# Adding two bias vectors on TensorE and redrawing five instruction lists in a two-layer transformer kernel

## What is computed

```python
gamma1, gamma2, scale1, scale2, shift1, shift2 = (silu(cond) @ Wada.T + bada)   # 6 x 256
def attn(xin):                                        # 16 heads of 16
    qkv = xin @ Wqkv.T + concat([q_bias, 0, v_bias])
    qn, kn = q / |q| * exp(min(s, log 100)), k / |k|
    p = softmax(qn @ kn.T + attn_bias)
    return (p @ v) @ Wproj.T + bproj
x = x + attn(ln(x) * (scale1 + 1) + shift1) * gamma1
h = gelu((ln(x) * (scale2 + 1) + shift2) @ Wfc1.T + bfc1)        # 1024 wide
x = x + (h @ Wfc2.T + bfc2) * gamma2
```

## Time and profile before

| what | us |
|---|---|
| median of 3 runs | 243.81 (243.23 to 246.11) |
| the profiled execution | 244.3 |
| its span, first to last instruction | 242.4 |
| DVE busy in the span | 201.6 |
| ACT busy | 156.6 |
| POOL busy | 95.3 |
| PE busy / PEld busy | 228.3 / 175.6 |

### The profile page before, as it was taken

How to read it: one execution, slowest core, us unless ns; L and a number is a source line. 1 busy time by engine, 2 the same in 40 slices (tenths; PEclk the granted TensorE clock), 3 DMA queues, 4 the chain that set the end, 5 groups by cost and what they waited for, 6 DMA issues and landing times.

```text
span 242.4 us, 4991 instructions
## 1 busy us (share of the span) xinstructions
PE 228.3 (94%) x1792; PEld 175.6 (72%) x1792; DVE 201.6 (83%) x418; ACT 156.6 (65%) x316; POOL 95.3 (39%) x167
## 2 busy tenths in 40 slices
PE   6999999999999999999999999999999799998982
PEld 2679674575567758567689999999897476867762
DVE  3879889999996997997977998776898988998743
ACT  2430491854899987985989828753608695877930
POOL 7416317028203302380839194234505545550000
PEclk9797999999999999999999999999999999999998
DMA  6970040000000003203000100000000000000112
GB/s 209 329 302 3 1 173 1 3 1 5 3 0 9 0 3 96 85 0 105 34 3 0 47 0 0 3 0 3 0 0 4 0 0 1 3 0 0 47 43 92
DMA packets 3641, 9.75 MB, mean 40 GB/s; under 512 B 536, under 2 KB 920, under 8 KB 3360
## 3 DMA queue, kind: packets, MB, share of 16 engines
q1 hardware_dynamic: 3616, 9.41, 11.3%
...
## 4 chain that ended last, share of the span: by engine, by line
PE 65%; DVE 15%; ACT 6%; issue 5%; POOL 3%; DMA 3%; SPq 1%; POOLq 0%; ACTq 0%; DVEq 0%
PE ring L835 11%; PE ring L841 10%; PE ring L836 10%; PE ring L837 10%; PE pv L944 5%; DVE nm L1223 5%; PE psx L974 5%; PE ring L898 3%; PE pv L1133 2%; PE psx L924 2%; DVE qn L1356 2%; DMA stage_a<-in_wada 2%; PE ring L848 1%; PE psx L1105 1%; DVE qstk L1397 1%
## 5 line engine op out<-in xcount | busy, mean ns | idle before, releaser
L1223 DVE TENSOR_REDUCE nm<-ring 128x2 f32<-128x512 f32 x64 | 40.2, 684 | 1.3 <-PE ring L898 0.8
L620 ACT ACTIVATE ps<-psx 128x1024 f32<-128x1024 f32 x32 | 31.4, 1026 | 6.0 <-PE psx L924 5.9
L835 PE MATMUL ring<-wqkv_hi,xm_hi 128*128 128x512 f32 (+1 forms) x64 | 24.2, 379 | 0.2
L974 PE MATMUL psx<-ident_b 128*128 128x512 bf16 x66 | 21.4, 449 | 2.0 <-POOL ones L477 2.0
L836 PE MATMUL ring<-wqkv_lo,xm_hi 128*128 128x512 f32 (+1 forms) x64 | 22.0, 343 | 0.0
L837 PE MATMUL ring<-wqkv_hi,xm_lo 128*128 128x512 f32 (+1 forms) x64 | 22.0, 343 | 0.0
L898 PE MATMUL ring<-kstk,qstk 64*128 64x256 f32 x128 | 19.4, 327 | 1.9 <-DVE nm L1223 1.6
L734 ACT ACTIVATE ps<-ring,col 128x256 f32<-128x256 f32 x32 | 13.3, 476 | 11.8 <-PE ring L837 11.2
L898 PEld LDWEIGHTS ring<-kstk,qstk 64*128 64x128 f32 x128 | 12.3, 184 | 10.5 <-DVE nm L1223 5.9
L490 POOL TENSOR_TENSOR nt<-ss,rn 128x64 f32<-128x64 f32 (+1 forms) x24 | 7.1, 296 | 32.3 <-DVE rn L1183 31.1
L574 POOL TENSOR_TENSOR stage_a<-qk,rope_sb 128x512 f32<-128x512 f32 x8 | 11.3, 1408 | 19.9 <-ACT qk L757 19.8
...
## 6 DMA issues: line engine op xcount, KB each, us to landing
...
row<-in_rows SPq DMA_DIRECT2D x1, 394.0 KB, 8.0
```

What stands on the lines that cost most here:

```text
L620: a.activation(ps[:, n % 4], psx[:, n % 2], ACT.Exp).then_inc(exp_done, 1)
L835: mm(dst, lhs[0], rhs[0], start=start, stop=False)
L974: mm(psx[:, 0, 0], ident_b[:, :], ident_b[:, :].unsqueeze(1).to_broadcast([P, 4, P]), start=True, stop=True)
L1223: v.tensor_reduce(nm[:, :, par, p], bank(key).rearrange("p (q n) -> p q n", q=TB), AX.X, ALU.max, negate=True).then_inc(ring_dve, 1)
```

## The change

The bias of q and of v is added by TensorE: a tile `mean`, 1/128 everywhere, is multiplied with the bias row, copied to all 128 partitions and split in hi and lo (`bias_parts`), between the matmuls of a product. That is two matmuls of 256 columns more for each of 8 tiles of q and k, and two for each of 8 half banks of v. ScalarE then empties the 8 `qk` and 4 `v` banks with a plain copy. In `heads0` ScalarE only makes hi, and VectorE takes lo straight out of PSUM and frees the bank. The sum of squares of the second layer's norm goes from VectorE's `stats2` to ScalarE (Square with a sum, two a batch). GpSimd adds epsilon in all 12 norms, in a step of its own. GpSimd's four late subtractions are cut in pieces of 512 columns. All five lists are new; there are again 33 `busy` steps.

```diff
-R_QK, R_V, R_PF, R_SML, R_SC = 0, 512, 768, 1280, 1296
-R_END = 1300
-R_KZERO = C
+R_PF, R_SML, R_SC = 512, 1024, 1040
+R_END = 1044
+V_BY_VECTOR = ()
 FILL = 2
+PIECE = 512
...
 SYNC_ORDER = steps("""
-load_w1 shift0:0 shift0:1 shift0:2 load_w2 shift0:3 load_wqkv1 load_wout1 proj1:0 proj1:1 proj1:2 proj1:3
+shift0:0 load_w1 shift0:1 shift0:2 shift0:3 load_w2 load_wqkv1 load_wout1 proj1:0 proj1:1 proj1:2 proj1:3
 """)
...
     if name == "qk0":
-        return [(("qk", tiles[i]), "dve")]
+        return [(("qk", tiles[i]), "act")]
     if name == "v0":
-        return [(("v", b), "dve")]
+        return [(("v", b), "dve" if b in V_BY_VECTOR else "act")]
...
     if name == "heads0":
-        return [(("aT", b), "act")]
+        return [(("aT", b), "dve")]
...
             def rstd_of(kind, b):
-                pool.wait_ge(stats_ready, stat_no[(kind, b)] + 1)
+                if kind < 2:
+                    pool.wait_ge(stats_ready, stat_no[(kind, b)] + 1)
+                    step(g.tensor_scalar(ve[:, kind, b, :], mv[:, kind, b, :, 1], LN_EPS, None, ALU.add))
+                else:
+                    pool.wait_ge(squares_summed, TB * (b + 1))
+                    step(g.tensor_scalar(ve[:, kind, b, :], mv[:, kind, b, :, 1], 1.0 / C, LN_EPS, ALU.mult, ALU.add))
...
+            def take_lo(lo, whole, hi):
+
+                for n in range(0, whole.shape[1], PIECE):
+                    ins = g.tensor_tensor(lo[:, n:n + PIECE], whole[:, n:n + PIECE], hi[:, n:n + PIECE], ALU.subtract)
+                ins.then_inc(w_lo_p, 1)
...
+                if name == "split_bias":
+                    pool.wait_ge(bias_hi, 1)
+                    g.tensor_tensor(bias_parts[:, 1, :], row[:, 0:2 * C], bias_parts[:, 0, :], ALU.subtract)\
+                     .then_inc(bias_lo, 1)
...
                 act.wait_ge(*full(key))
                 act.wait_ge(*full(read_before))
-                src = bank(key).rearrange("p (f n) -> p f n", f=FC)
-                a.activation(at[:, :, :], src, ACT.Copy)
-                a.activation(at_hi[:, :, :], src, ACT.Copy).then_inc(ring_act, 1)
+                a.activation(at_hi[:, :, :], bank(key).rearrange("p (f n) -> p f n", f=FC), ACT.Copy)\
+                 .then_inc(heads0_hi, 1)
...
+                if name == "split_bias":
+                    act.wait_ge(s_row, 32)
+                    a.activation(bias_parts[:, 0, :], row[:, 0:2 * C], ACT.Copy).then_inc(bias_hi, 1)
+                if name == "qk0":
+
+                    t = TB * b + i_
+                    act.wait_ge(*full(("qk", t)))
+                    if t >= TB:
+                        act.wait_ge(qn_ready, t - TB + 1)
+                    a.activation(qk[:, t % TB, :], bank(("qk", t)), ACT.Copy).then_inc(ring_act, 1)
...
+                if name == "stats2":
+                    act.wait_ge(x3_ready, b + 1)
+                    for i in range(TB):
+                        if b or i:
+                            act.wait_ge(squares_summed, TB * b + i)
+                        a.activation(junk[:, :], xs[:, TB * b + i, :], ACT.Square,
+                                           accum_out=mv[:, 2, b, i, 1:2])\
+                         .then_inc(squares_summed, 1)
...
+            def add_bias(dst, first):
+
+                mm(dst, mean[:, :], bias_parts[:, 0, first:first + C], start=False, stop=False)
+                mm(dst, mean[:, :], bias_parts[:, 1, first:first + C], start=False, stop=False)
...
+                    if kind == 0 and f == 1:
+                        if (b, i) == (0, 0):
+                            pe.wait_ge(mean_ready, 1)
+                            pe.wait_ge(bias_lo, 1)
+                        add_bias(dst[:, 0:C], 0)
...
-                if name == "qk0":
-                    t = TB * b + i_
-                    dve.wait_ge(*full(("qk", t)))
...
-                    v.tensor_tensor(qk[:, t % TB, :], bank(("qk", t)), row[:, R_QK:R_QK + 2 * C], ALU.add)\
-                     .then_inc(ring_dve, 1)
...
                 if name == "unit0":
                     t = TB * b + i_
                     dve.wait_ge(rn_ready, b + 1)
+                    dve.wait_ge(*emptied(("qk", t)))
```

More of the change, by code:

```diff
@@ new lines @@
+busy:24 max0:0.1 busy:25 max0:0.2 busy:26 normed0:3 qk0:2.0 max0:0.3 busy:27 busy:28 max0:0.4 qk0:2.1 max0:0.5
+busy:29 busy:30 max0:0.6 busy:31 turnq0:1.0 turnq0:1.1 busy:19 max0:0.7 busy:20 turnk0:1.0 turnk0:1.1 shift0:0
+gamma:2 max0:1.0 busy:21 busy:22 max0:1.1 busy:23 max0:1.2 score0:0.0 score0:0.1 qk0:3.0 score0:0.2 max0:1.3
+value0:0.0 score0:0.3 score0:0.4 max0:1.4 qk0:3.1 max0:1.5 score0:0.5 value0:0.1 score0:0.6 max0:1.6 gamma:3
+value0:0.2 max0:1.7 score0:0.7 turnq0:2.0 out0:0.0 shift0:1 value0:0.3 turnk0:2.0 turnq0:2.1 turnk0:2.1 out0:0.1
@@ L294, in build @@
         rstd = sb("rstd", [P, 3, B, TB])
+        junk = sb("junk", [P, C])
         zero_col = sb("zero_col", [P, 1])
@@ L961, in project @@
             def project(key, n, w):
-                pe.wait_ge(at_ready, n + 1)
+                if n < B:
+                    pe.wait_ge(*emptied(("aT", n)))
+                else:
+                    pe.wait_ge(at_ready, n - B + 1)
                 dst = claim(key)
@@ L1335, in _ @@
                         dve.wait_ge(v_const, 1)
[L1336 to L1340 removed]
+                    v.tensor_copy(vs[:, b % 3, :, :, 0:D0], bank(("v", b)).rearrange("p (t a d) -> p t a d", t=TB, d=D0))\
+                     .then_inc(ring_dve, 1)
                 if name == "sums0":
```

197 lines of the change are left out of this document (94 added, 103 removed).

## The result

The changed kernel takes 245.41 us in the median of 19 runs (244.38 to 248.73), the kernel before 243.75 (242.54 to 246.65): a ratio of 1.0069, 95% interval 1.0046 to 1.0091. It is 1.7 us slower, where 5.1 us of gain were forecast. The profiled execution took 245.02 us, its span 243.2. (The profiled execution of one experiment, `hold_clock`, took 248.01 us, above its median of 245.38; only lengths of single stages are taken from it.)

The account below looks back on a forecast made before the run. VectorE was taken to matter up to about 135 us with TensorE close behind, TensorE to be full in the MLP. Gains of 6.1 us less 1.0 for matmuls made 5.1: 238.7 us median, range 233.0 to 246.0.

Parts of the forecast that it names:

- The four stretches: Row maxima, 37.90 to 110.60: VectorE nearest its limit, so its relief gains 1.4, 1.5, 0.8 and 0.7 us.
- the 1.0 for matmuls: Charge for 32 added bias matmuls, 3.8 us on TensorE, mostly hidden beside busy matmuls or where VectorE leads.
- Behind the maxima: From 110.60 on: 0.7 us gained to 135, 0 in the MLP where TensorE is full, 0.5 behind 182.
- The term of 0.7 in the fourth stretch: From 92.65 to 110.60: a normalisation moves out and ScalarE loses the hi part of w1, gaining 0.7 us.
- the 0.7 to 135: From 110.60 to 135: a v pair leaves VectorE and GpSimd's pieces relieve w2, together gaining 0.7 us.
- The opening: Before the first row maxima at 37.91: VectorE sheds work, but other chains stay nearly where they were, gaining 0.5 us.
- the milder form of "TensorE had set the pace": Rival: ScalarE's 4.8 us and the matmuls eat most of VectorE's relief, 241.5 to 246; little or nothing gained had chance 0.20.
- VectorE alone: Rival: VectorE alone had set the pace to about 135, so its whole relief returns, 232 to 236 us; chance 0.19.
- ScalarE's queue: Rival: q, k and v banks wait behind ScalarE's exponentials and hold up TensorE, 249 us and more; chance 0.11.
- The signs named: Changed profile: VectorE at most 92% busy from first maxima to 110, `shift0:1` some 3 us sooner, GpSimd's pieces near 1.2 us.
- three signs of failure: TensorE waiting over 3 us for ScalarE's q, k, v copies; first q and k product awaiting bias; MLP growing from ScalarE's squares.

Follow-up runs that it names:

- hold_clock: Changed kernel plus eight 512-column matmuls, product never read, in TensorE's 1.89 us gap in the second layer: 245.38 us, ratio 1.0052 to the kernel before.
- vector_bias: Changed kernel with VectorE again emptying the q, k and v banks and adding the biases, no bias matmuls or ScalarE copies of these banks: 248.46 us, ratio 1.0196.
- w1_early: Changed kernel with ScalarE's hi part of w1 moved back between two exponentials of batch 2, as before the change: 243.78 us, ratio 0.9975 to the kernel before.
- turn_w1: Changed kernel with the hi part of w1 early again and one set of second-layer transposes put back earlier, both bias matmuls kept: 243.95 us, ratio 0.9974.

## Why the prediction was wrong

**The four stretches, 4.4 us less a share of the 1.0 for matmuls: measured 0.95.** Two terms were wrong. The relief was taken nearly whole, 1.4 + 1.5 + 0.8 + 0.7; the ladder shows 0.9 from before to `vector_bias` (the mask, the additions of epsilon and all else that differs, not taken apart) and 1.27 for the banks, 2.2 in all. And the matmuls, charged with 1.0 us for all 32 because the later half "lie where VectorE leads", cost 1.20 of their 1.4 us in this stage alone. (The earlier half lies before the first maxima at 37.90, and not before 55.60 as the prediction has it; its 1.9 us for the rest is right.) Each step was right about who led before; the sum went past the point at which TensorE leads. The rule of the Trainium skill that the prediction weighed (Perfetto Trace Analysis, Identifying the Most-Contended Engine), to judge by weight loads, said that TensorE had room: weight loads fill 46.74 of 71.32 us there. The matmul row, 69.21 of 71.32, was the better sign, and the measurement decides.

**Behind the maxima, 0.7 + 0 + 0.5 gained: measured 2.2 lost to `proj0:3`, 1.1 gained in the MLP, 1.9 lost in the second layer.** This is the larger miss, 4.2 us, and a step left out and not a size. The term of 0.7 in the fourth stretch counted that "ScalarE loses the hi part of w1" and did not follow the moved step: GpSimd's four pieces wait for it and now stand, 5.46 us long, in front of the root of `norm1:1`. Undone, 0.93 of the 2.2 come back. Of the 1.26 that remain in `w1_early`, some 0.6 is `gelu:1.0`, which crossed the mark, and four bias matmuls of `v0:3` make 0.48 at 0.12 each: with the split early the scaling of `proj0:2` comes 13.64 us behind `shift0:3`, before it came at 13.13, and one matmul for two takes 0.23 off the stage (28.22 to 27.99). With the late split these matmuls cost nothing (29.17 without them, 29.21 with them), since the root held TensorE up there anyway. The relief by pieces that the 0.7 to 135 counted on was real (0.6 at w2). The second layer's order was not walked at all ("1.1 us or more a batch off VectorE"); of its 1.9 the runs show that the old lists bring it back, and not which step does.

**The opening, 0.5 gained: not measurable.** The profile shows 1.2, but the same instructions take 36.4 to 40.2; the middle of the ten is 37.7, and before's one profile, 37.91, had its own half clock (0.50 from 10 to 12 and from 20 to 22).

With that middle the changed kernel sums to 37.7 + 206.0 to 206.5 + 1.8 = 245.5 to 246.0, near the median of 245.41.

**The rivals.** The time lies in the milder form of "TensorE had set the pace", 241.5 to 246, given a part of 0.20; its mechanism holds in the maxima, but that alone would have left a gain of 0.95. What brought the time there is a loss behind the maxima that no rival had, so that it lies inside the stated 233.0 to 246.0 is luck. "VectorE alone" and "ScalarE's queue" fell. **The signs named:** VectorE is under 92% in three of the four stretches (96% in the first); `shift0:1` comes 2.2 us sooner, not 3; ScalarE is busy 14.63 and 16.31 us in the middle two; the pieces of w1 and w2 take 1.4 to 1.5 us in the mean, and no subtraction of VectorE's for the gelu is over 2.0 (the longest 1.80). Of the three signs of failure one came in part: the first q and k product waits for the bias, in some profiles not at all (`w1_early`), in others 0.28 to 0.92 us. The longest is that of `turn_w1`:

```profile
13.67 0.36 PE L908 MATMUL ring<-bias_parts,mean 128*128 128x256 f32 x1 [0.92 <-POOL bias_parts L516]
```

The forecast had GpSimd's part of it at 1.15 us, and it takes 1.27 to 1.78. The other two signs stayed away, and the larger failure lay where none was named.
